# Filler matmuls ahead of the output gate and in the steps of a table load, and FFN norms in two VectorE operations

## What is computed

```python
x = x + deformable_conv(group_norm(x))       # 3x3, learned offsets, 256 places per image
t = tokens(x)                                # 4 x 256 tokens of 64
t = t + attn(layer_norm(t))                  # 8 heads of 32, then the FFN below
t = t + cell(layer_norm(t))                  # 256 steps in sequence, batch 4, width 64
# inside attn, with y the projected heads:
x1 = layernorm(y + x, ln1_g, ln1_b)
ff = (gelu(y @ w1.T) * (y @ wv.T)) @ w2.T
out = layernorm(ff + x1, ln2_g, ln2_b)
# one cell step; note h * c, not f * c: the forget gate isn't used
i_t = sigmoid(xi_t + h @ V_i); g_t = tanh(xg_t + h @ V_c); o_t = sigmoid(xo_t + h @ V_o)
c = h * c + i_t * g_t
h = o_t * tanh(c)
```

## Time and profile before

| | us |
|---|---|
| median of 3 runs | 446.27 (445.75 to 447.76) |
| the profiled execution | 446.74 |
| its span, first to last instruction | 444.6 |
| mean granted clock of PE in it | 0.942 |
| busy: PE, DVE, ACT, POOL | 405.4, 242.6, 270.1, 68.2 |
| first new state `H` written | 108.55 |
| last new state written | 442.14 |

### The profile page before, as it was taken

The page is one execution under the profiler, slowest core; times in us unless marked ns, Lnnn a source line. Parts: engine busy times, 40 slices in busy tenths (PEclk is TensorE's granted clock), DMA queues, the critical chain, the costliest instruction groups (busy, mean ns, idle before and its releaser), DMA issues.

```text
span 444.6 us, 14683 instructions
## 1 busy us (share of the span) xinstructions
PE 405.4 (91%) x5607; PEld 217.2 (49%) x5607; DVE 242.6 (55%) x1144; ACT 270.1 (61%) x1142; POOL 68.2 (15%) x164
## 2 busy tenths in 40 slices
PE   7999989886998899889989998999899889988896
PEld 2655544553554455445545554555455535543332
DVE  2577743443656455656555654565446546664443
ACT  1766644662774677478657856685667567753443
POOL 6000004012212011301031111121112111120000
PEclk9999998996999689989998998699869989999999
DMA  7000000000000000000000000000000000000000
GB/s 231 0 1 3 0 1 0 1 1 0 4 4 2 5 1 4 1 5 3 3 1 4 4 1 2 4 4 3 1 6 1 4 2 4 4 2 5 1 1 5
DMA packets 2243, 3.76 MB, mean 8 GB/s; under 512 B 1277, under 2 KB 1726, under 8 KB 2174
## 3 DMA queue, kind: packets, MB, share of 16 engines
q1 hardware_dynamic: 1872, 2.32, 1.7%
q10 hardware_dynamic: 302, 0.52, 0.4%
HBM read 2.57 MB, written 0.26 MB: 6 GB/s over the span
## 4 chain that ended last, share of the span: by engine, by line
PE 64%; ACT 16%; DVE 13%; issue 5%; POOL 1%; DMA 1%; DVEq 0%
PE bank L361 15%; PE bank L633 15%; PE bank L490 8%; DVE bank L1022 5%; ACT SA L757 5%; PE bank L428 5%; PE bank L416 5%; PE bank L501 4%; DVE H L1032 4%; ACT L746 4%; ACT bank L764 4%; PE bank L518 3%; PE bank L389 2%; ACT E L734 1%; PE bank L555 1%
## 5 line engine op out<-in xcount | busy, mean ns | idle before, releaser
L361 PE MATMUL bank<-FB 128*128 128x512 bf16 (+2 forms) x615 | 178.4, 382 | 1.2 <-DVE FB L790 1.2
L633 PEld LDWEIGHTS bank<-H,VW 128*32 128x32 f32 x3072 | 55.2, 113 | 111.3 <-DVE H L1032 106.9
L633 PE MATMUL bank<-H,VW 128*32 128x4 f32 x3072 | 77.7, 182 | 24.6 <-DVE H L1032 14.3
L757 ACT ACTIVATE SA<-bank 64x8 f32<-64x8 f32 x256 | 44.5, 174 | 89.3 <-PE bank L633 87.8
L1022 DVE TENSOR_TENSOR_SCAN bank<-SA 64x12 f32<-64x12 f32 x256 | 49.5, 193 | 80.9 <-ACT SA L757 79.4
L1032 DVE SCALAR_TENSOR_TENSOR H<-TO,bank 64x4 f32<-64x4 f32 x256 | 40.9, 160 | 42.9 <-ACT bank L764 39.6
L361 PEld LDWEIGHTS bank<-FB 128*128 128x128 bf16 x615 | 45.8, 100 | 25.4 <-issue 6.8
L335 POOL TENSOR_SCALAR E<-E,rinv 128x256 f32<-128x256 f32 x56 | 26.8, 478 | 160.1 <-DVE rinv L913 160.1
L490 PE MATMUL bank<-KF,QB 128*128 128x256 f32 x128 | 48.4, 464 | 1.6 <-DVE rinv L913 1.2
L764 ACT ACTIVATE bank<-bank 64x4 f32<-64x4 f32 x256 | 38.4, 150 | 17.9 <-DVE bank L1022 1.9
L761 ACT ACTIVATE TO<-bank 64x4 f32<-64x4 f32 x256 | 43.6, 170 | 6.2
(11 more groups left out here) (120 smaller groups left out, 354.8 us busy)
## 6 DMA issues: line engine op xcount, KB each, us to landing
AW<-in_attn_w SPq DMA_DIRECT2D x1, 768.5 KB, 8.2
DW<-in_dcn_w SPq DMA_DIRECT2D x1, 576.0 KB, 6.8
X<-in_x_fm SPq DMA_DIRECT2D x1, 256.0 KB, 3.3
X<-in_x_fm ACTq DMA_DIRECT2D x1, 256.0 KB, 5.5
out_dram<-OUT SPq DMA_DIRECT2D x8, 32.0 KB, 1.5
CW<-in_conv_w SPq DMA_DIRECT2D x1, 243.5 KB, 4.3
VEC<-in_vecs SPq DMA_DIRECT2D x1, 160.0 KB, 8.1
K<-in_consts ACTq DMA_DIRECT2D x1, 154.0 KB, 3.5
```

The lines of the kernel that those rows point to most:

```text
L361: nc.tensor.matmul(idle[:, 0:n], FB[:, 0:P], FB[:, 0:n], start=True, stop=True)
L633: mm = nc.tensor.matmul(gate_out(m, gate, r, slice(B * s, B * (s + 1))), VW[:, gate, r], H[:, (g - 1) % RING, :], start=False, stop=True, ...
L757: nc.scalar.activation(SA[:, 0, :, 1:3].rearrange("p b g -> p g b"), b_cell[m % 2][0:C, 0:2 * P].rearrange("p (g s b) -> p g s b", g=2, b= ...
```

## The change

Five things, all in the order of the work:

1. In each cell step PE now does the input and cell gates, then up to 256 columns of filler (`COLS_PART`), then the output gate, then the rest of the filler.
2. In the steps behind a table load (`switched`, steps 20 and 30) `planned` is lowered by 900 ns and `MOST` doesn't hold, so the filler there grows: from 896 to 2944 columns in step 20, from 384 to 2560 in step 30. Ahead of the first step the filler of steps 26 to 30 grows from 512 to 1536 columns each.
3. The FFN norms lose their two POOL operations each and the DVE operation of two scalars. In their place DVE does `(r - mean) * gain` and `r * inverse root + bias`, both as scalar_tensor_tensor.
4. The product of GELU and gate, and the matmul behind it (`NARROW`), move from step 24 to 25, the sum behind them (`NARROWED`) from 25 to 26. The statistics of the second norm move to step 26 ahead of the scan, their aggregation behind the scan.
5. The copy of the cell's turned input (`XT`) moves from behind the scan of step 30 to ahead of the scan of step 31.

```diff
@@ -53,11 +53,12 @@
 GELU = 23
-NARROW = 24
-NARROWED = 25
-STATS = (22, 25, 28)
+NARROW = 25
+NARROWED = 26
+STATS = (22, 26, 28)
 AGGR = (23, 26, 28)
-NORM = (24, 27, 29)
+CENTRED = (24, 27)
+SCALED = (24, 28, 29)
 CELL_INPUT = 30
@@ -71,8 +72,10 @@
 NS_FILL = 54
+NS_TABLE = 900
 MOST = 3 * 512
 COLS_EARLY = 512
+COLS_PART = 256
 
@@ -220,8 +223,7 @@
                              "t_rs", "t1_done", "ln3_done", "xt_mm", "xt_done"))
-        x1_norm, x1_gain, x1_done, r2_norm, r2_gain = (sem(n) for n in (
-            "x1_norm", "x1_gain", "x1_done", "r2_norm", "r2_gain"))
+        centred, x1_done = sem("centred"), sem("x1_done")
         st_done = sem("st_done")
@@ -341,16 +343,6 @@
                         inverse_root(m, AGGR.index(o))
-                    if o == NORM[0]:
-                        pool.wait_ge(x1_norm, m + 1)
-                        nc.gpsimd.tensor_tensor(X1[:], X1[:], VEC[:, VEC_G1, :], ALU.mult).then_inc(x1_gain, 1)
-                        pool.wait_ge(x1_gain, m + 1)
-                        nc.gpsimd.tensor_tensor(X1[:], X1[:], VEC[:, VEC_B1, :], ALU.add).then_inc(x1_done, 1)
-                    if o == NORM[1]:
-                        pool.wait_ge(r2_norm, m + 1)
-                        nc.gpsimd.tensor_tensor(R2[:], R2[:], VEC[:, VEC_G2, :], ALU.mult).then_inc(r2_gain, 1)
-                        pool.wait_ge(r2_gain, m + 1)
-                        nc.gpsimd.tensor_tensor(T1[:, m, :], R2[:], TB[:, m, :], ALU.add).then_inc(t1_done, 1)
 
@@ -582,6 +574,10 @@
 
+            def switched(g):
+
+                return any(o in (EXP_TABLE + 1, GELU_TABLE + 1) for _, o in at(g))
+
             def planned(g):
@@ -590,7 +586,7 @@
                     ns += NS_INPUT * (o == CELL_INPUT) + NS_PRELOAD * (o == CELL_READY)
-                return ns + NS_STATES * (leaving(g) is not None)
+                return ns + NS_STATES * (leaving(g) is not None) - NS_TABLE * switched(g)
 
@@ -623,22 +619,31 @@
 
+            def gate_sums(m, s, gate):
+                for r in (slice(0, HC), slice(HC, C)):
+                    mm = nc.tensor.matmul(gate_out(m, gate, r, slice(B * s, B * (s + 1))), VW[:, gate, r],
+                                          H[:, (STEPS * m + s - 1) % RING, :], start=False, stop=True,
+                                          skip_group_check=True)
+                return mm
+
             for g in EVERY:
...
                         pe.wait_ge(h_done, g)
-                    for gate in range(3):
-                        for r in (slice(0, HC), slice(HC, C)):
-                            mm = nc.tensor.matmul(gate_out(m, gate, r, slice(B * s, B * (s + 1))), VW[:, gate, r], H[:, (g - 1) % RING, :],
-                                                  start=False, stop=True, skip_group_check=True)
-                        if gate == 1:
-                            mm.then_inc(ig_mm, 1)
-                    mm.then_inc(o_mm, 1)
-                    if g < LAST - 1:
-                        fill(min(MOST, P * ((NS_STEP - planned(g)) // NS_FILL)), b_cell[(m + 1) % 2])
+                    gate_sums(m, s, 0)
+                    gate_sums(m, s, 1).then_inc(ig_mm, 1)
+                    idle = b_cell[(m + 1) % 2]
+                    cols = P * ((NS_STEP - planned(g)) // NS_FILL)
+                    if not switched(g):
+                        cols = min(cols, MOST)
+                    if g == LAST - 1:
+                        cols = 0
+                    fill(min(cols, COLS_PART), idle)
+                    gate_sums(m, s, 2).then_inc(o_mm, 1)
+                    fill(cols - COLS_PART, idle)
                 elif start(0) + WEIGH_AT[0] < g < start(0) + CELL_READY:
-                    fill(COLS_EARLY, b_cell[1])
+                    fill(COLS_EARLY if g < start(0) + NARROWED else MOST, b_cell[1])
                 beside(g)
@@ -937,6 +942,19 @@
 
+            def centre(m, j, r, gain):
+
+                dve.wait_ge(t_mv, 3 * m + j + 1)
+                nc.vector.scalar_tensor_tensor(out=r, in0=r, scalar=mv[:, j, 0:1], in1=VEC[:, gain, :],
+                                               op0=ALU.subtract, op1=ALU.mult).then_inc(centred, 1)
+
+            def scale(m, j, dst, r, bias):
+
+                dve.wait_ge(centred, 2 * m + j + 1)
+                dve.wait_ge(t_rs, 3 * m + j + 1)
+                return nc.vector.scalar_tensor_tensor(out=dst, in0=r, scalar=rs[:, j, :], in1=bias,
+                                                      op0=ALU.mult, op1=ALU.add)
+
             def beside_gates(g):
@@ -958,8 +976,10 @@
                         norm_aggr(m, 0)
-                    if o == NORM[0]:
-                        norm_apply(m, 0, X1[:], R1[:]).then_inc(x1_norm, 1)
+                    if o == CENTRED[0]:
+                        centre(m, 0, R1[:], VEC_G1)
+                    if o == SCALED[0]:
+                        scale(m, 0, X1[:], R1[:], VEC[:, VEC_B1, :]).then_inc(x1_done, 1)
                     if o == NARROW:
@@ -969,13 +989,20 @@
                         nc.vector.tensor_tensor(R2[:], b_t[:, 0:C], X1[:], ALU.add).then_inc(r_done, 1)
-                    if o == AGGR[1]:
-                        norm_aggr(m, 1)
-                    if o == NORM[1]:
-                        norm_apply(m, 1, R2[:], R2[:]).then_inc(r2_norm, 1)
+                    if o == STATS[1]:
+                        dve.wait_ge(r_done, 2 * m + 2)
+                        norm_stats(m, 1, R2[:])
+                    if o == CENTRED[1]:
+                        centre(m, 1, R2[:], VEC_G2)
+                    if o == SCALED[1]:
+                        scale(m, 1, T1[:, m, :], R2[:], TB[:, m, :]).then_inc(t1_done, 1)
                     if o == STATS[2]:
...
                         norm_stats(m, 2, T1[:, m, :])
+                    if o == CELL_READY:
+                        dve.wait_ge(xt_mm, m + 1)
+                        nc.vector.tensor_copy(XT[0:C, m, :, :].rearrange("p t b -> p (t b)"), b_t[0:C, 0:P]
+                                              ).then_inc(xt_done, 1)
                 if leaving(g - 1) is not None:
@@ -994,17 +1021,12 @@
                         norm_stats(m, 0, R1[:])
-                    if o == STATS[1]:
-                        dve.wait_ge(r_done, 2 * m + 2)
-                        norm_stats(m, 1, R2[:])
+                    if o == AGGR[1]:
+                        norm_aggr(m, 1)
                     if o == AGGR[2]:
                         norm_aggr(m, 2)
-                    if o == NORM[2]:
+                    if o == SCALED[2]:
                         norm_apply(m, 2, LN3[:], T1[:, m, :]).then_inc(ln3_done, 1)
-                    if o == CELL_INPUT:
-                        dve.wait_ge(xt_mm, m + 1)
-                        nc.vector.tensor_copy(XT[0:C, m, :, :].rearrange("p t b -> p (t b)"), b_t[0:C, 0:P]
-                                              ).then_inc(xt_done, 1)
```

## The result

| | before | after |
|---|---|---|
| median, us | 447.01 (445.75 to 448.33, 4 runs) | 465.39 (465.16 to 466.49, 4 runs) |
| ratio to before | | 1.0416 [1.0377, 1.0454] |
| the profiled execution, its span | 446.74, 444.6 | 465.34, 463.2 |
| mean granted clock in it | 0.942 | 0.995 |
| first `H`, last `H` | 108.55, 442.14 | 107.48, 460.77 |

The kernel got slower by 18.4 us; 460 was predicted, in a range of 440 to 479. First the page of the kernel after: busy time of the engines, the granted clock in 40 slices, the chain that ended last, and the filler's group.

What follows compares the result with a forecast made beforehand. The cell's chain over PE, ACT and the scan was taken to set the pace, not PE. Terms +27.8 + 4.4 + 4.7 - 17.5 - 1.7 - 1.0 - 2.6 = +14.1 gave about 460 us, range 440 to 479.

Steps and rivals of the forecast that it cites:

- split: last tile: In the 31 steps of the last tile, the split makes each 0.115 us longer: +3.6 us.
- split: pairs, 7 in each of 7 tiles: In steps 5 to 18, the split costs 0.115 us a step, and odd steps 0.09 more: +15.7 us.
- split: the rest: In the other steps of the seven tiles, 0.115 us each plus extras in crowded and table steps: +17.6 us.
- split in all: Over all cell steps, filler ahead of the output gate costs +36.9 us.
- table filler, clock: More filler stops clock falls behind step 30 (-17.5 us) and ahead of the first step (-1.7): -19.2 us.
- norms and moves: Shorter norms and the moved product save 1.0 us ahead of the first step and 2.6 in steps 24 to 27.
- the third at 0.89 instead of 0.77: In a plain step, the late output gate delays ACT's third tanh by 0.12 us, by finer reading 0.115.
- Odd crowded steps: In odd steps 5 to 17, PE's chain takes 1.38 us against 1.29 for the cell chain: 49 x 0.09 = +4.4 us.
- 0.37 is PE's own: In odd crowded steps, the last 0.37 us are PE's work; were it waiting for `H`, the +4.4 would be 0.
- Table steps: Step 20 takes 2.30 us against 2.11 (+0.19); steps 30 and 31 together +0.19, with ACT's query copies late.
- the clock falls too: Rival: in the longer cell steps low clock stretches return as often as now, the 19.2 us stay: 479 us; chance 0.14.
- Norms: Ahead of the first step, -0.88 us in the second norm, -0.09 in the first; steps 24 to 27, -0.38 a tile.

Runs made afterwards that it cites:

- Experiment 7: Filler ahead of the output gate made with 32 columns of weights instead of 128, still 256 columns streamed, against the kernel after: 427.49 us, ratio 0.9620.
- experiment 2: The kernel after without the split (COLS_PART 0 instead of 256), parts 2 to 5 kept: 426.55 us, ratio 0.9559.
- experiment 3: Only the added filler in table steps and ahead of the first step (part 2), on the kernel before: 431.05 us, ratio 0.9661.
- experiments 1 and 10: 1: the split alone on the kernel before, 596.43 us. 10: the kernel after without the added table filler (part 2), 591.83 and 515.53 us.
- experiment 8: In steps with the turned input and queries, that work put ahead of the filler, against experiment 2: 425.99 us, ratio 0.9588.

## Why the prediction was right, and where a size was off

The direction and the cause were right: part 1 adds two gaps of 0.10 us to each step, and this outweighs what the filler of the table steps gives back. The gaps themselves were read well. In the kernel after, 0.105 us lie between the last gate matmul and the filler (510 times) and 0.10 to 0.11 between the end of 256 filler columns and the next gate weights (of 335 times, 0.11 in 255 and 0.10 in 72). Experiment 7 shows the first to be the price of the tile's shape, and takes both away. By which path the gaps are paid was wrong for the plain step, as the next points say, and that the split came out at 38.8 against 36.9 is luck in part.

| term | predicted | measured, and from what |
|---|---|---|
| split: last tile | +3.6 (31 x 0.115) | +2.6, experiment 2 |
| split: pairs, 7 in each of 7 tiles | +15.7 (49 x (2 x 0.115 + 0.09)) | +18.7 (steps 5 to 18 of all tiles, against experiment 2) |
| split: the rest | +17.6 | +17.4 in the tiles |
| split in all | +36.9 | +38.8 by medians |
| table filler, clock | -19.2 | -15.9, experiment 3 |
| norms and moves | -3.6 | -4.5, experiment 2 against 3 (-2.6 in the rows of the norms) |
| sum | +14.1 | +18.4 |

- **The step that failed** is the one by which "the third at 0.89 instead of 0.77" sets a plain step. The prediction took 0.20 us as the least distance between two tanh on ACT. That distance was seen behind a tanh of 8 columns only; the third followed the second by 0.08 in plain steps, and `H` came 0.04 late. What a plain step pays is PE's own work, which the prediction didn't sum for such a step: filler from 0.61, 1280 columns and a gap, 1.25. By its own times (output gate at 0.40 to 0.44) the sum would have been about 1.2, so under the 1.29 that it had for the chain, and it would have looked hidden. Its times are 0.06 short of the 0.61 at which the second piece begins: it took the eighth matmul at 0.09, where it starts among twelve, but eight by themselves get there at 0.12, and the output gate's four take 0.06 and not 0.04. Two errors met here, and their difference is small: 0.08 us a step were measured, 0.115 predicted. The forecast of 40 us for the last tile came out as 38.87.
- **Odd crowded steps.** The sum on PE was 1.38, and 1.45 was measured: the output gate's weights load at 0.44 and not at 0.40, and its filler starts at 0.60, for the same reason. The assumption that "0.37 is PE's own" held: the load waits for "issue" in the odd step after. In the even steps the third tanh is 0.19 behind the second, and 1.31 was measured for 1.29.
- **Table steps.** Predicted were 2.30 for step 20, and 0.19 more for 30 and 31 together. From gates' load to gates' load step 20 takes 2.43, and 30 and 31 take 2.24 + 1.52 where they took 2.24 + 1.17 at full clock, 0.35 more. From `H` to `H`, as in the table above, 20 and 30 are both 2.10, and PE's excess comes out a step later: 21 takes 1.54 us and 31 takes 1.70. The queries on ACT were named as the cause for 31; 0.21 us of it are there without the split (1.38 in experiment 2 against 1.17 before), and 0.32 come with it.
- **The clock.** The falls behind step 30 and the one right ahead of the first step are gone, as predicted; the one stretch left in the kernel after is from 66.0 to 69.4 us, where the earlier trace rows have a dip as well. Yet the first `H` comes only 1.1 us earlier, where 2.7 were predicted (1.7 for the clock, 1.0 for norms). The traces differ by up to 1.6 us ahead of any change (the first aggregation of the FFN norms stands at 97.5 to 99.1), so the two are better read from the aggregation of the first FFN norm on. From the third norm's row to the first `H` written, 3.83 us became 3.09: 0.74 for the clock and the filler ahead of the first step, not 1.7. In the seven tiles experiment 3 gives back 15.7 of the predicted 17.5, and the fall that was left costs 1.2. The gain of 15.9 us includes 0.08 us a tile that the longer filler costs in steps 30 and 31. The kernel before had medians of 443 to 449 us where it was run beside the experiments, depending on where its clock fell, so that 3 us of difference in this term are within what its own runs vary by.
- **The rival "the clock falls too"** was priced at 479 with 0.14. Its premise, that longer steps could lose the clock, is what experiments 1 and 10 show, and far more than its price: it took each fall to be as long as today's, and the four that were traced lasted 81.9 to 283.3 us, against 10.2 at most. It didn't come to pass because part 2 was in the same change.
- **Norms.** Ahead of the first step -1.0 was predicted and -0.5 measured. The rows are the aggregation of the first norm and the third norm, first of the kernel before, then of the kernel after, and between them the second norm of the kernel after:

```profile
97.85 0.18 DVE L934 BATCH_NORM_AGGREGATE mv<-st 128x2 f32<-128x6 f32 x1
104.73 0.31 DVE L938 TENSOR_SCALAR LN<-T,mv,rs 128x64 f32<-128x64 f32 x1 [0.99 <-POOL rs L330]
```
```profile
98.03 0.18 DVE L939 BATCH_NORM_AGGREGATE mv<-st 128x2 f32<-128x6 f32 x1
102.63 0.28 DVE L955 SCALAR_TENSOR_TENSOR T<-R,rs,TB 128x64 f32<-128x64 f32 x1 [0.85 <-POOL rs L332]
102.95 0.23 DVE L935 BATCH_NORM_STATS2 st<-T 128x6 f32<-128x64 f32 x1
104.39 0.31 DVE L943 TENSOR_SCALAR LN<-T,mv,rs 128x64 f32<-128x64 f32 x1 [0.99 <-POOL rs L332]
```

  From the first aggregation to the third norm, 6.88 us became 6.36. The second norm did go from 1.14 to 0.32 us. But from each of the first two aggregations to the row that applies the inverse root, 1.20 us became 1.35, since the inverse root on POOL took 0.32 instead of 0.23 beside DVE's new operation: +0.15 in the first norm where -0.09 was predicted, and +0.15 in the second.

  In steps 24 to 27 -0.30 us a tile for the -0.38 predicted. The `XT` copy gave back 0.13 us in step 30 (2.24 to 2.11), and step 31 took as much more (1.25 in experiment 3, 1.38 in experiment 2): no gain from part 5 by itself. With the queries ahead of the filler step 31 is at 1.19 (experiment 8).

## What to carry to other kernels

Filler matmuls between small ones cost more than their columns when their weights have another tile shape: here 0.10 us on entry and 0.10 on exit, in nearly every one of 256 steps. Small matmuls that ran beside others at no cost can cost their own time once they stand alone: 0.06 us here for the output gate. Give the filler the shape of its neighbours (experiment 7), or leave one block of it a step. When an edit adds work or gaps to the engine that was second in line, sum that engine's whole step too, plain steps included; the bound can change hands. And test a filler's effect on the clock together with the edits that lengthen the steps: the same split cost 38.8 us beside all other parts and 149.5 (119 to 169) without them.

## What the runs showed of the hardware that was not expected

- Once fallen, the granted clock stayed at 0.50 for 82 to 283 us in the kernels with the split and no table filler, with PE busy for 97% of the stretch, and for 3.4 to 10.2 us in the kernel before. What ends such a stretch isn't known from these runs; all four that were traced ended by themselves. Each began ahead of the first `H` or behind a step 30.
- The distance between the second and the third tanh on ACT was 0.08 us in most steps of the kernel after, and 0.19 in steps behind an exponent whose accumulator is read. The trace shows this together and doesn't show that the one causes the other.
- With 256 of a step's filler columns in a tile of 32 columns of weights and the rest in full tiles, the clock held: 0.998 in experiment 7. A kernel with narrow filler alone wasn't run.
- In experiment 7 the output gate's matmuls start ahead of those of the narrow filler that stands before them in the program: the matmul that signals `o_mm` starts 0.12 us into the step, the filler at 0.15. The signal itself comes at 0.47, where without that filler it comes at 0.38.
